# Graph attention on one core: score, value and transpose work regrouped by two pairs of heads, with seven banks used in turn

## What is computed

```
xn = layernorm(x);  xg = layernorm(xn) * g + b
q, k, v = xg @ Wq + bq, xg @ Wk + bk, xg @ Wv + bv          # (1250, 8, 64)
ws  = sum(q[src] * k[dst], -1) / 8 * edge_weights           # one score for each edge and head
e   = exp(ws - segment_max(ws, src)[src])
att = e / segment_sum(e, src)[src]
val = segment_sum(att * v[dst], src)                        # (1250, 512)
gnn = xn + (val @ W1 + b1) @ W2 + b2
mix = linear attention of xn (elu features, four products, Wp)
x   = x + gnn + mix
x   = x + ffn(layernorm(x))                                 # integer digits in columns 128 to 159
```

## Time and profile before

| | |
|---|---|
| runs shown | 802.64 us median (800.6, 802.64, 811.86) |
| profiled execution | 803.23 us, span from first to last instruction 801.5 us |
| PE busy | 736.1 us (92%) |
| DVE, ACT, POOL busy | 563.7, 388.2, 401.3 us |
| attention, group 0 (352.7 to 484.5 us) | 131.8 us for 40 units |
| attention, group 1 (484.5 to 620) | 135.5 us for 40 units |
| attention, group 2 (620 to 775) | 155.0 us for 40 units |
| end (775 to 801.5) | 26.5 us |

### The profile page before, as it was taken

One profiled execution on the slowest core, in us unless ns is written; L12 is line 12 of the kernel. 1 busy time (PEld: TensorE's weight loads), 2 busy tenths in 40 slices (PEclk: granted clock), 3 DMA queues, 4 the chain that ended last, 5 costly groups with the idle time before them and its releaser, 6 DMA issues.

```text
span 801.5 us, 13739 instructions
## 1 busy us (share of the span) xinstructions
PE 736.1 (92%) x4643; PEld 446.3 (56%) x4682; DVE 563.7 (70%) x1295; ACT 388.2 (48%) x917; POOL 401.3 (50%) x399
## 2 busy tenths in 40 slices
PE   1997798898999999979999999999999999999984
PEld 0543345544445654436666666666666876667662
DVE  4468767684223252349998998999999887788696
ACT  0411110122130223117777777878788866566561
POOL 1007777777777777777777777875000000001030
PEclk9999799998999999999999999999999999999996
DMA  7779886798755588104444444435552323422203
GB/s 233 196 272 328 316 301 243 241 337 293 246 183 183 178 297 295 39 5 148 175 150 173 154 170 158 164 119 213 161 202 79 138 94 123 150 97 92 93 1 128
DMA packets 69636, 143.66 MB, mean 179 GB/s; under 512 B 22187, under 2 KB 54251, under 8 KB 65599
## 3 DMA queue, kind: packets, MB, share of 16 engines
q1 hardware_dynamic: 47084, 119.42, 41.5%
q10 hardware_dynamic: 9136, 17.39, 6.6%
q0 software_dynamic: 13344, 5.92, 4.0%
HBM read 77.99 MB, written 64.80 MB: 178 GB/s over the span
## 4 chain that ended last, share of the span: by engine, by line
PE 76%; DVE 8%; SPq 6%; DMA 4%; ACT 3%; issue 2%; ACTq 1%; another core or an unknown queue 0%; DVEq 0%
PE bank L942 16%; PE bank L1176 12%; PE bank L1139 12%; PE bank L1158 11%; PE bank L936 9%; SPq L435 5%; PE bank L1204 4%; PE bank L1149 3%; DMA V<-in_edge_attr_dram 3%; PE bank L1182 2%; PE bank L1049 2%; DVE AR L1604 2%; PE bank L1000 1%; DMA kv_rows<-AR 1%; DVE lstat L1662 1%
## 5 line engine op out<-in xcount | busy, mean ns | idle before, releaser
L536 POOL DMA_INDIRECT w_tab<-pay,idx x330 | 340.6, 1032 | 154.5 <-issue 99.9
L1139 PE MATMUL bank<-KT,QT 64*128 64x512 f32 (+1 forms) x480 | 116.4, 562 | 4.4 <-DVE AR L1593 2.5
L1176 PE MATMUL bank<-AR,V 128*64 128x128 f32 (+1 forms) x1600 | 114.4, 281 | 0.0
L795 ACT ACTIVATE AR<-AR,nmx 128x512 f32<-128x512 f32 (+1 forms) x160 | 105.7, 662 | 14.4 <-DVE nmx L1608 14.4
L936 PE MATMUL bank<-AR 128*128 128x512 f32 (+1 forms) x288 | 106.1, 527 | 4.7 <-ACT QT L667 2.8
L942 PE MATMUL bank<-AR 128*128 128x512 f32 x240 | 108.1, 606 | 2.5 <-ACT AR L723 2.5
L1604 DVE CUSTOM_DVE_ANT_0 AR<-bank,AR,MX 128x512 f32<-128x512 f32 (+1 forms) x106 | 100.9, 990 | 9.3 <-remote 4.3
L609 POOL DMA_INDIRECT AR<-kv_rows,xd x10 | 10.6, 1063 | 179.3 <-PE bank L1176 159.2
L1176 PEld LDWEIGHTS bank<-AR,V 128*64 128x64 f32 (+1 forms) x1600 | 85.2, 137 | 20.6 <-issue 20.6
L803 ACT ACTIVATE bank<-AR 128x512 f32<-128x512 bf16 (+1 forms) x89 | 49.0, 551 | 78.0 <-DVE MX L1604 76.9
L936 PEld LDWEIGHTS bank<-AR 128*128 128x128 f32 x288 | 54.5, 192 | 51.6 <-issue 45.9
(11 more groups left out here) (267 smaller groups left out, 974.7 us busy)
## 6 DMA issues: line engine op xcount, KB each, us to landing
w_tab<-ztile SPq DMA_DIRECT2D x20, 2280.0 KB, 14.5
AR<-w_tab SPq DMA_DIRECT2D x20, 2048.0 KB
AR<-w_tab SPq DMA_DIRECT2D x10, 1344.0 KB
w_tab<-ztile SPq DMA_DIRECT2D x3, 1800.0 KB, 13.6
w_tab<-pay,idx POOLq DMA_INDIRECT x330
w_tab<-ztile SPq DMA_DIRECT2D x2, 1700.0 KB, 8.8
kv_rows<-AR ACTq DMA_DIRECT2D x9, 256.0 KB, 6.4
kv_rows<-V ACTq DMA_DIRECT2D x9, 256.0 KB
```

The costliest lines, as they stand in the source:

```text
L536: pool.indirect_dma_start(out=w_tab, out_offset=bass.IndirectOffsetOnAxis(ap=idx[:, k, j:j + 1], axis=0), in_=pay[:, k % RING, j, :], in_o ...
L795: act.activation(ws[u % 3][hh][:, 0:n], ws[u % 3][hh][:, 0:n], ACT.Exp, bias=nmx[:, u % 4, hh:hh + 1], accum_out=DG[g][:, c, 2 * p + hh:2 ...
L1139: last = mm(bs[hh][:, 0:m], qs[hh], KT[64 * hh:64 * hh + 64, p, d0:d0 + m], start=not over, stop=over and g < 2, skip_group_check=over)
L1176: last = mm(bank[4 + w % 2][64 * hh:64 * hh + 64, p * P:(p + 1) * P], v, PT[u % 2][hh][0:rws, i * P:(i + 1) * P], start=(i == 0), stop=(i ...
```

## The change

The loops of PE, ACT and DVE no longer go over u but over d = 0 to 59, two units at a time: units 2d and 2d + 1, with d = 2w + q.

- PE's iteration d is: scores of both units, then the masks of the heads that are not laid, all together, then the extra work (inverse, factor, W1·W2, collided rows), then values of units 2d - 4 and 2d - 3, and last the transposes of units 2d - 2 and 2d - 1.
- Seven banks go round. Every use of a bank by scores (s), transposes (t), factor (f), inverse (r), W1·W2 (y) and collided rows (l) has a number in PE's order (`USES`), takes bank number mod 7, and waits until the use seven before it has been read. Values have the eighth bank alone, so a w's values wait for the w before it to be taken.
- Laid are now (u odd, head 1) and (p = 2, head 0): again three of eight a w. `lay_mask` of d + 1 stands on ACT after the copies for d - 1 and the exponentials of unit 2d.
- `on_act`: in group 0 the odd copy of p = 1 goes to ACT (none before); in groups 1 and 2 those of p = 0, 1 and 2 (before p = 0 and 1).
- `PT` is four units deep; `fo` moves to the memory of `pay`.
- On DVE the digits of the first eight tiles (`bits(0)`, `digits(0)`, `finish(0)`) stand behind the loop, between the additions for tiles 8 and 9.

```
 def on_act(u):
-    return u // 4 >= NT and u % 4 in (0, 1)
+    return u % 4 in (0, 1, 2) if u // 4 >= NT else u % 4 == 1
-def laid(u):
-    return u >= 2 and u % 4 != 0
+def laid(u, hh):
+    return (hh == 1 and u % 2 == 1 and u > 4) or (hh == 0 and u % 4 == 2 and u > 4)
+def four(d):
+    return [(2 * d + i // 2, i % 2) for i in range(4)]
...
+        def use(what):
+            return bank[USE_OF[what] % NB][:, :]
+        def free(eng, what):
+            r = USE_OF[what]
+            if r >= NB:
+                eng.wait_ge(s_bk[r % NB], r // NB)
+        def gone(eng, what):
+            r = USE_OF[what]
+            eng.wait_ge(s_bk[r % NB], r // NB + 1)
...
# ACT
-            def lay_mask(u):
+            def lay_mask(u, hh):
                 act.wait_ge(s_pen, w + 1)
-                act.wait_ge(s_ttr, 2 * u - 2)
-                act.activation(bank[SB[2 * u % 3]][:, 0:n], pen[w % 2][:, 0:n], ACT.Copy).then_inc(s_laid, 1)
+                free(act, ("s", u, hh))
+                act.activation(use(("s", u, hh))[:, 0:n], pen[w % 2][:, 0:n], ACT.Copy).then_inc(s_laid, 1)
...
-            for u in range(NU + 8):
-                if 2 <= u <= NU + 1:
-                    even_probs(u - 2)
-                if u + 2 < NU and laid(u + 2):
-                    lay_mask(u + 2)
-                if u < NU:
-                    exps(u)
...
+            for d in range(ND + 1):
+                if q == 0 and 2 <= w <= NT + 1:
+                    keep(w - 2)
+                if q == 0 and NT <= w - 1 < NW:
+                    change(w - 1)
+                if q == 0 and 2 * NT <= w - 2 < NW - 1:
+                    inverse(w - 2)
+                if q == 1 and 2 * NT <= w + 1 < NW:
+                    loser_k(w + 1)
+                if d >= 1:
+                    for u in (2 * d - 2, 2 * d - 1):
+                        probs(u, 0)
+                        if on_act(u):
+                            probs(u, 1)
+                if d < ND:
+                    exps(2 * d)
+                    if d + 1 < ND:
+                        for u, hh in four(d + 1):
+                            if laid(u, hh):
+                                lay_mask(u, hh)
+                    exps(2 * d + 1)
...
# PE
+            for d in range(ND + 4):
+                w, q = d // 2, d % 2
+                if d < ND:
+                    scores(d)
+                if q == 0 and 2 * NT <= w - 2 < NW - 1:
+                    inverse(w - 2)
+                if q == 1 and NT <= w - 1 < NW:
+                    factor(w - 1)
+                if d == ND + 1:
+                    values(NU - 2)
+                    values(NU - 1)
+                    inverse(NW - 1)
+                if q == 1 and 2 * NT <= w - 2 < NW:
+                    ffn(w - 2)
+                if q == 1 and 2 * NT <= w + 1 < NW:
+                    loser_k(w + 1)
+                if 2 <= d <= ND:
+                    values(2 * d - 4)
+                    values(2 * d - 3)
+                if 1 <= d <= ND:
+                    transposes(d - 1)
...
# DVE
+            for d in range(ND + 3):
+                if q == 0 and NT <= w - 1 < NW:
+                    change(w - 1)
+                if q == 0 and NT <= w - 2 < NW:
+                    merged(w - 2)
+                if q == 0 and 2 * NT <= w - 2 < NW:
+                    scaled(w - 2)
+                if d < ND:
+                    weighted(2 * d, 0)
+                    weighted(2 * d, 1)
+                if 1 <= d <= ND:
+                    odd_probs(2 * d - 2)
+                if d < ND:
+                    shift_of(2 * d)
+                if q == 1 and NT <= w - 1 < NW:
+                    rescaled(w - 1)
+                if d < ND:
+                    weighted(2 * d + 1, 0)
+                if q == 1 and w + 1 < NW:
+                    mask(w + 1)
+                if d < ND:
+                    weighted(2 * d + 1, 1)
+                if 1 <= d <= ND:
+                    odd_probs(2 * d - 1)
+                if d < ND:
+                    shift_of(2 * d + 1)
+                if q == 0 and NT <= w - 1 < NW:
+                    denominators(w - 1)
+                if q == 1 and 2 * NT <= w - 2 < NW - 2:
+                    added(w - 2)
+            bits(0)
+            added(NW - 2)
+            digits(0)
+            finish(0)
+            added(NW - 1)
+            bits(1)
+            digits(1)
+            finish(1)
```

312 lines of the change are left out of this document (142 added, 170 removed).

## The result

The changed kernel takes 952.7 us (median of runs from 949.5 to 955.8) where the kernel before takes 805.4 (800.6 to 811.9): a ratio of 1.182, with a 95% interval of 1.172 to 1.192. The profiled execution has a span of 949.9 us, against 801.5.

What follows compares the result with a forecast made beforehand. PE's list was taken to bound the attention. From 801.5 us, -26 (shape changes), +126 (waits), +3 (end) and +68 (clock) gave 972.5, with about 1 for executions 973 us; range 885 to 1090.

Steps and rivals of the forecast that it cites:

- waits as counted and a clock that falls now and then: Whole kernel: the forecast case, 973 us, in its own range of 920 to 1050; chance 0.45.
- Shape changes: PE in the attention: fewer changes of array shape at 0.15 us each, 0.3 us saved per d, -26 us with the extras.
- The chain over ACT: Even d, group 0: PE's scores wait for ACT's copy, exponentials and laid mask behind the transposes, 2.3 us idle.
- The chain over DVE: Odd d, group 0: scores wait for DVE's weighting behind odd_probs, 1.3 us, then 0.45 more, together 1.75.
- keep: Group 0: values wait for the eighth bank, which ACT empties only after exps(2d + 1), 0.8 us a w.
- Group 2: Group 2 waits before scores: 1.8 us in even d (ACT), 2.0 in odd d (product's bank); 38 us over ten w.
- The end: Behind the last scores: moved digits and tile 8's addition cost +5 us, a wait of 2.0 falls away; +3 us.
- The clock: PE's granted clock halves in one of three of 60 waits, 3.4 us late each; +68 us, bounds 0 and +204.
- the clock holds: Rival for the whole kernel: the chain waits as counted, but the clock stays up; 906 us, chance 0.26.
- it falls almost always: Rival for the whole kernel: the clock falls after almost every pause; 1110 us, chance 0.16.
- Half of it: Rival on PE's waits before scores: 1.2 us each, with the clock kept; 852 us, chance 0.06.
- Faster: Rival: masks laid in time, seven banks absorb the pauses, only saved shape changes left; 780 us, chance 0.04.

Runs made afterwards that it cites:

- e_fill: Changed kernel plus extra f32 matmuls on PE into an already free bank ahead of the scores of odd d; 933.7 us, ratio 1.158 to the kernel before.
- e_tfirst_lay: Changed kernel with PE's transposes before values, ACT's masks laid early in even d, DVE's weighting ahead of its odd copy; 832.9 us, ratio 1.031 to the kernel before.
- e_extras_late: e_tfirst_lay with factor, product and collided rows behind the transposes in odd d, ring renumbered to match; 811.8 us, ratio 1.006 to the kernel before.
- e_scaled_late: e_extras_late with DVE's scaled(w - 2) behind unit 2d's weightings; on a slower chip 1154.0 us against 1168.5 before, ratio 0.989, repeat 1.000.
- e_before_digits: Kernel before with only bits(0) moved on DVE behind the last scaled, ahead of digits(0); ratios 0.996 and, repeated, 1.011 to the kernel before.

## Why the prediction was right, and where it was not

The case that was forecast, waits as counted and a clock that falls now and then, is the one that came, and 952.7 us lies in its own range (920 to 1050). That 973 is only 20 us off is luck in part: in the table below, the clock and group 0 came out 52 us under the prediction, and the rest 28 us over it.

| | predicted | measured |
|---|---|---|
| group 0, clock apart | 42.5 | 34.7 |
| group 1, clock apart | 32.5 | 36.7 |
| group 2, clock apart | 26 | 36.6 |
| behind the last scores, clock apart | 3 | 12.8 |
| clock | 68 | 24 |
| part ahead of the attention | 0 | 3.7 |

The clock's 24 is an estimate: 2 falls in group 0 and 8 in group 1 at 1.6 each (a w of group 1 takes 17.4 to 17.5 us without, 19.1 with one and 20.7 to 20.9 with two), 20.5 us low in group 2 at 0.2 (e_fill), and half of the 7.6 us that are low in addition behind the last scores. In the predicted column the waits and the savings of each group are taken together, with rounding.

**Shape changes (right).** The waits of a w in group 0 come to 4.66 us and the w grew by 3.90, so two iterations saved 0.76: 0.38 per d for 0.3 predicted. e_tfirst_lay gives a second reading, from its two lines above. Its w has six changes less than before's and takes 12.98 us; its scores reach the next group after 2.32 and 2.09 us, where 1.92 is enough without a wait (429.92 to 431.84 in the changed kernel). Without these 0.57 us it would be 12.41 for 13.33: 0.15 for each change, as predicted. The Trainium skill (TensorEngine Tiling (Array Packing), Key Properties) says that a change of tiling mode drains the engine; the saving agrees, though by that rule alone the kernel would have become faster.

**The chain over ACT (right).** In even d 2.3 us were predicted; the trace has 2.14, plus the 0.16 by which a group's modelled end lies behind the start that the next could have. Step by step: copy, exponentials and mask were to end at 0.33, 1.74 and 2.34 us after the last transpose; they end at 0.25, 1.65 and 2.25.

**The chain over DVE (right).** In odd d 1.3 and 0.45 were predicted, 1.22 and 0.68 measured.

**keep (too high).** 0.8 us a w were predicted and 0.30 + 0.16 = 0.46 came: 3.4 us over ten w. I had also counted the first w of group 0, where no mask is laid as yet, as one like the others, for 4.25; it took 12.46 us for 11.03 before, with a fall of the clock in it. These two are most of the 8 us by which group 0 fell short.

**Group 1 (a little low).** A w grew from 13.92 to 17.43 to 17.50 us, 3.5, for the predicted 3.25.

**Group 2 (the step that failed in the waits).** A w undisturbed by the clock grew from 15.76 to 20.30 us, 4.5; the prediction had 2.6. The 2.6 are 1.8 + 2.0 of waits less 1.2 saved; that sum treated the banks of the ring as always free, but for one. PE in one w of group 2 of the kernel after:

```profile
840.72 0.65 PE L1183 MATMUL bank<-KT,QT 64*128 64x226 f32 x4 [1.80 <-ACT bank L842]
849.78 0.52 PE L1204 MATMUL bank<-ident,AR 128*128 128x128 f32 x3 [0.68 <-DVE MX L1649]
850.89 0.52 PE L1204 MATMUL bank<-ident,AR 128*128 128x128 f32 x3 [0.58 <-DVE MX L1649]
851.75 0.65 PE L1183 MATMUL bank<-KT,QT 64*128 64x226 f32 x4 [0.35 <-DVE XRES L1712]
853.53 0.65 PE L1183 MATMUL bank<-KT,QT 64*128 64x226 f32 x4 [0.92 <-ACT bank L842]
855.62 0.66 PE L1229 MATMUL bank<-ident,AR 128*128 128x128 f32 x4 [0.70 <-ACT AR L869]
```

The 1.80 (and 0.16) is the predicted chain of 1.8, a little longer. But the 0.68 and 0.58 are transposes whose banks had the second pair of this iteration's scores, seven uses back since three extra uses lie between, and wait for DVE to read them; and the 0.70 is the turned inverse, whose copy ACT makes behind the laid masks and exponentials that PE's own pauses have made late. Both were missed. The 2.0 us that I gave to the product's bank (L1712) are 0.35, and 0.92 for the mask behind it. e_extras_late bears this out, in the order of e_tfirst_lay: moving the extra uses behind the transposes took 2.1 us from each w of group 2, 0.5 from those of group 1, which has the factor alone, and nothing from those of group 0, which has no extra work. How the 4.5 us divide in the changed kernel itself is read from these lines; no run takes its waits away one by one.

**The end (the second step that failed).** I had priced only the digits, +5, and the wait of 2 that falls away, and got +3. From the start of the last product to the end the estimate was good: 15.6 us before (785.87 to 801.5) and 5 more are 20.6, and 21.5 were measured (928.40 to 949.9). The rest is that more work is left when the last scores have gone, since the values now follow two iterations later: 150 matmul records and 24.6 us of PE, for 99 and 17.8 before. Two waits lie in it. PE and DVE at the end of the kernel after:

```profile
916.29 1.12 PE L1229 MATMUL bank<-ident,AR 128*128 128x128 f32 x4 [3.85 <-ACT AR L869]
927.65 0.69 DVE L1707 TENSOR_TENSOR AR<-bank,AR 128x512 f32<-128x512 f32 x1 [3.54 <-PE bank L1247]
928.40 3.70 PE L1247 MATMUL bank<-AR 128*128 128x512 f32 x8 [0.88 <-DVE AR L1707]
```

From the last scores to the end of the last scaling it takes 26.0 us for 15.3 before, and the 3.85 us for the inverse are part of it. e_scaled_late, with few of the attention's stalls left, still has 10.8 us more behind its last scores. Of these 2.6 are what moving the digits costs by e_before_digits. The other 8 or so go with the work left over by the deeper pipeline; that is argued from the counts above, since no run has a shallower one.

**The clock (a term mis-sized).** This is the step that failed most: 68 us were predicted and some 24 came. For the 60 waits 20 falls were predicted and 15 came up to the last scores, so the count was fair. The size was not. I took 6.8 us low for each from two falls in rows 10 (the trace of before has a longer one too, 10.2 us from 79.0, which they leave out), and 16 of 17 lasted 3.4, as in the three stretches above; that halves the term. What was left cost 1.6 us each in groups 0 and 1 and less in group 2, where PE waits for others anyhow. The Trainium skill (TensorE: Matmul & The Clock Gate, A second HAM failure mode: psum-queue depth-cycling) tells of a clock that swings because PE idles briefly between groups. The runs agree: e_fill shortened every second pause, with the waits ending when they did, and 18 falls became 7. The section gives no count; the fall after nearly every pause, for which the prediction took it, did not come: 15 in 60.

**Rivals.** That the clock holds (906 us) is ruled out by the clock column; that it falls almost always (1110) by the same. *Half of it* (852) is out as well: in even d of group 0 PE waited 2.14 us, not 1.2. *Faster* fell at the laid masks, as its own condition says. What it could have given is seen in e_scaled_late: with nearly every chain covered the attention is 11.5 us shorter, not 26, and the end takes it back.
